# The inverse-total product of the pair attentions moved from VectorE to GpSimd, with shorter runs of unused products

## The reference

```
x = x + attn_a0(norm(x))     16 heads of 64, one key and one value head for all, no mask
x = x + ffn(norm(x))         FP6 blocks of 32, 128 x 128 weight, bias
x = x + attn_a1(norm(x))     16 heads of 64, causal
x = x + ffn(norm(x))
x = x + attn_a2(norm(x))     16 heads over a latent of 32, causal
x = x + experts(norm(x))     top 2 of 8 experts and a shared one
x = x + attn_a3(norm(x))     16 heads of 64, causal, with biases
x = x + experts(norm(x))
attn: softmax(q k^T / 8) v, then the output projection
```

## Time and profile before

| what | value |
|---|---|
| time, median of 3 runs | 2546.32 us (2542.83 to 2547.62) |
| time of the profiled execution | 2549.15 us |
| its span, first to last instruction | 2547.4 us |
| mean granted TensorE clock | 0.982 |
| PE busy | 2461.7 us (97%) |
| DVE busy | 1508.9 us (59%) |
| ACT busy | 1217.3 us (48%) |
| POOL busy | 1263.0 us (50%) |

### The profile page before, as it was taken

The page is one execution under the profiler, slowest core; times in us unless marked ns, Lnnn a source line. Parts: engine busy times, 40 slices in busy tenths (PEclk is TensorE's granted clock), DMA queues, the critical chain, the costliest instruction groups (busy, mean ns, idle before and its releaser), DMA issues. The chain is left out here.

```text
span 2547.4 us, 49159 instructions
## 1 busy us (share of the span) xinstructions
PE 2461.7 (97%) x20265; PEld 1306.2 (51%) x20265; DVE 1508.9 (59%) x2062; ACT 1217.3 (48%) x1830; POOL 1263.0 (50%) x824
## 2 busy tenths in 40 slices
PE   7999999999999999999998999999989999999989
PEld 4444444444444455445546666666554555455545
DVE  5666656777555665556654667666454555555544
ACT  4544545544545555454552344444335554455541
POOL 3877777777766663656543000000006555655530
PEclk9999999999999999999998989999999999999989
DMA  3000000000000000000001100000000000000000
GB/s 85 1 1 1 1 1 1 1 1 1 1 1 1 1 1 1 1 1 1 1 1 23 35 2 3 3 3 3 1 1 1 1 1 1 1 1 1 1 1 17
DMA packets 18658, 13.05 MB, mean 5 GB/s; under 512 B 3074, under 2 KB 17795, under 8 KB 18308
## 3 DMA queue, kind: packets, MB, share of 16 engines
q1 hardware_dynamic: 18436, 9.92, 1.5%
HBM read 8.87 MB, written 1.05 MB: 4 GB/s over the span
## 5 line engine op out<-in xcount | busy, mean ns | idle before, releaser
L1590 POOL TENSOR_TENSOR sums<-sums,p 128x1024 f32<-128x1024 f32 (+3 forms) x384 | 818.8, 2132 | 359.4 <-PE ps L1217 316.2
L1411 DVE TENSOR_REDUCE half_max<-ps 128x2 f32<-128x1024 f32 (+3 forms) x384 | 442.3, 1153 | 381.3 <-PE ps L1196 344.1
L1308 ACT ACTIVATE p<-ps 128x1024 f32<-128x1024 f32 (+3 forms) x384 | 347.7, 916 | 223.3 <-PE ps L1173 164.9
L1170 PE MATMUL ps<-q,k 64*128 64x512 f32 (+3 forms) x1792 | 428.2, 556 | 0.0
L918 POOL TENSOR_TENSOR sums<-sums,p 128x1024 f32<-128x1024 f32 (+3 forms) x160 | 277.5, 1735 | 182.8 <-PE ps L651 166.5
L1217 PE MATMUL ps<-p,v 128*64 128x512 f32 (+3 forms) x1536 | 336.9, 553 | 0.0
L1173 PE MATMUL ps<-max_row,pick 64*128 64x512 f32 (+3 forms) x896 | 326.4, 725 | 0.0
L816 DVE TENSOR_REDUCE half_max<-ps 128x2 f32<-128x1024 f32 (+3 forms) x128 | 130.1, 1019 | 155.2 <-PE ps L630 121.6
L1844 ACT ACTIVATE p<-ps 128x2048 f32<-128x2048 f32 (+1 forms) x80 | 136.5, 1707 | 169.5 <-PE ps L1737 92.0
L1196 PE MATMUL ps<-k_near,q_near 64*128 64x512 f32 (+2 forms) x896 | 195.5, 434 | 21.1 <-DVE half_max L1411 19.2
L1196 PEld LDWEIGHTS ps<-k_near,q_near 64*128 64x128 f32 x896 | 84.6, 186 | 222.8 <-issue 124.5
(11 more groups left out here) (298 smaller groups left out, 4007.7 us busy)
## 6 DMA issues: line engine op xcount, KB each, us to landing
q_w<-in_wq SPq DMA_DIRECT2D x3, 512.0 KB, 5.4
o_w<-in_wo SPq DMA_DIRECT2D x3, 512.0 KB, 8.0
x<-in_x SPq DMA_DIRECT2D x4, 256.0 KB, 3.7
k_w<-in_wk SPq DMA_DIRECT2D x2, 512.0 KB, 6.7
v_w<-in_wv SPq DMA_DIRECT2D x2, 512.0 KB, 7.9
out<-x SPq DMA_DIRECT2D x4, 256.0 KB, 2.3
p<-in_wq_t SPq DMA_DIRECT2D x1, 512.0 KB, 5.1
p<-in_w_out SPq DMA_DIRECT2D x1, 512.0 KB, 7.2
```

The costliest lines, as they stand in the source:

```text
L1170: nc.tensor.matmul(out[:, head, 0:width], a.k[rows, owner(i) % 3, k * P:(k + 1) * P], a.q[rows, i % 3, s * BANK + lo:(s + 1) * BANK], star ...
L1308: act.activation(probabilities(g)[:, :, lo:BANK], score[g % 2][:, :, 0:BANK - lo], ACT.Exp)\
L1411: last = v.tensor_reduce(out, chunk_ps(c)[:, :, 0:hi - lo], AX.X, ALU.max, negate=True)
L1590: pool.tensor_tensor(sums, sums, probabilities(g)[:, :, lo:BANK], ALU.add).then_inc(summed, 1)
```

## The change

- `WARM` goes from 30 to 18, and the counts become: 18 in the opening; 30, 14 and 20 in the norm phase (from 60, 30, 30); 6 in the latent phase (from 15); 3 in each expert phase (from 4).
- In the norm phase POOL's bias addition waits for the quantised values.
- In the three pair attentions `normalise` leaves DVE's list and stands in POOL's, one step earlier, behind the `add_up` of that step. `inverse` has two buffers, so that DVE's spread waits for the product two units back.
- The values of the latent attention's batch 1 move from step 8 to step -3.
- In the expert phases the first gate and up products stand ahead of the router's products of groups 2 and 3.

```
-WARM = 30
+WARM = 18
...
-                pool.wait_ge(normed[g % 2], (g - first) // 2 + 1)
+                pool.wait_ge(quantised, g - first + 1)
...
-            keep_busy(2 * WARM)
+            keep_busy(30)
...
-            keep_busy(WARM)
+            keep_busy(14)
...
-                keep_busy(WARM)
+                keep_busy(20)
...
-                if u >= 1:
-                    dve.wait_ge(normed, u)
-                v.transpose(a.inverse[:].rearrange("p (b q) -> p b q", q=QB),
+                if u >= 2:
+                    dve.wait_ge(normed, u - 1)
+                v.transpose(a.inverse[:, u % 2, :].rearrange("p (b q) -> p b q", q=QB),
                             a.inverses[:].unsqueeze(2).to_broadcast([P, BANK // QB, QB])).then_inc(spread, 1)
-
-            def normalise(i, s):
-                u = unit(i, s)
-                dve.wait_ge(spread, u + 1)
-                dve.wait_ge(mixed_out, u + 1)
-                if u >= 1:
-                    dve.wait_ge(small_mm, use_of["out", (u - 1) // 2, (u - 1) % 2] + 1)
-                v.tensor_tensor(a.mixed[:], a.mixed_raw[:, u % 2, :], a.inverse[:], ALU.mult).then_inc(normed, 1)
...
-                    norms_at[at + 4] = (i, s)
...
-                if g in norms_at:
-                    normalise(*norms_at[g])
...
+            def normalise(i, s):
+                u = unit(i, s)
+                pool.wait_ge(spread, u + 1)
+                pool.wait_ge(mixed_out, u + 1)
+                if u >= 1:
+                    pool.wait_ge(small_mm, use_of["out", (u - 1) // 2, (u - 1) % 2] + 1)
+                pool.tensor_tensor(a.mixed[:], a.mixed_raw[:, u % 2, :], a.inverse[:, u % 2, :], ALU.mult)\
+                    .then_inc(normed, 1)
+
+            norms_at = {begins[i] + when(i)["total", s] + 4: (i, s) for i in range(ITEMS) for s in range(2)}
             for g in range(BEGIN, LAST + 1):
                 if 0 <= g - 1 < TOTAL and step(g - 1)[2] > 0:
                     add_up(g - 1)
+                if g in norms_at:
+                    normalise(*norms_at[g])
...
-                 (("k", 0, 0, -11), ("k", 0, 1, -6), ("v", 0, 0, -4), ("k", 1, 0, -2), ("k", 1, 1, 2), ("v", 1, 0, 8))]
+                 (("k", 0, 0, -11), ("k", 0, 1, -6), ("v", 0, 0, -4), ("v", 1, 0, -3), ("k", 1, 0, -2), ("k", 1, 1, 2))]
...
-                    for _ in range(WARM // 2):
+                    for _ in range(6):
...
-            keep_busy(0, 4)
+            keep_busy(0, 3)
             turn(0, 0)
             for g in range(1, GROUPS):
                 turn(0, g)
+                if g == GROUPS - 1:
+                    gate_and_up(0)
                 route(g - 1)
             route(GROUPS - 1)
-            for i in range(AHEAD - 1):
+            for i in range(1, AHEAD - 1):
```

More of the change, by code:

```diff
@@ L875, in _ @@
                     .then_inc(bias_scaled, 1)
-            turns_at, inverts_at, norms_at = {}, {}, {}
+            turns_at, inverts_at = {}, {}
             for i in range(ITEMS):
@@ L924, in _ @@
             bias_at = {-2: 0, 4: 1, 8: 2, 16: 3}
+            def normalise(i, s):
[6 more added lines that the diff above has]
+                    .then_inc(normed, 1)
+            norms_at = {i * NS + when["total", s] + 4: (i, s) for i in range(ITEMS) for s in range(2)}
             for g in range(BEGIN, LAST + 1):
@@ L1915, in invert @@
                         dve.wait_ge(normed, u)
-                v.reciprocal(a.inverse[:, cols], a.mixed_raw[:, u % 2, QW + half * P:QW + (half + 1) * P])\
+                v.reciprocal(a.inverse[:, 0, cols], a.mixed_raw[:, u % 2, QW + half * P:QW + (half + 1) * P])\
                     .then_inc(inverted, 1)
@@ L1963, in normalise @@
                     pool.wait_ge(small_mm, use_of["out", (u - 1) // UNITS, (u - 1) % UNITS] + 1)
-                pool.tensor_tensor(a.mixed[:, 0:QW], a.mixed_raw[:, u % 2, 0:QW], a.inverse[:, 0:QW], ALU.mult)\
+                pool.tensor_tensor(a.mixed[:, 0:QW], a.mixed_raw[:, u % 2, 0:QW], a.inverse[:, 0, 0:QW], ALU.mult)\
                     .then_inc(normed, 1)
@@ L2349, in build @@
         a.mixed_raw = sb("mixed_raw", [P, 2, BANK])
-        a.mixed, a.total, a.inverse = sb("mixed", [P, BANK]), sb("total", [P, BANK]), sb("inverse", [P, BANK])
+        a.mixed, a.total, a.inverse = sb("mixed", [P, BANK]), sb("total", [P, BANK]), sb("inverse", [P, 2, BANK])
         a.turned, a.inverses = sb("turned", [P, BANK]), sb("inverses", [P, BANK // QB])
```

## The result

| | before | changed kernel |
|---|---|---|
| median, first comparison | 2546.2 us (4 runs) | 2532.3 us (4 runs, 2530.48 to 2534.12) |
| ratio, 95% interval | 1 | 0.9947 (0.993 to 0.9965) |
| profiled execution, its span | 2549.15, 2547.4 us | 2532.78, 2531.0 us |

A second comparison with six more runs of the same changed kernel gave a ratio of 0.9935 (0.9921 to 0.9949). The ten runs of both have a median of 2531.6 us and lie between 2522.5 and 2534.1 us: this spread of 11.6 us is larger than any term of the forecast's sum.

The account below looks back on a forecast made before the run. In the steady part only PE's own work was taken to set the time, with idle or unused products at the joints. Terms -1 + 10 - 2.6 - 10.7 - 8.8 + 0 = -13.1 us gave a 2533.2 us median, range 2525 to 2541.

Parts of the forecast that it names:

- steady pair attentions: Product on POOL at 1.27 us costs 0, hidden; relieved DVE shortens row-maximum waits: 1 us gained, ends 0 and 6.
- two ends: Ends of stream and a3: POOL's products lengthen its addition chain and delay `total`, +5 us each, +10 us together.
- opening: Start of the kernel: 24 fewer rows of unused products, 2.6 us gained.
- norm phase: Shorter fills start DVE's addition at line 389 9.8 us earlier, last fill gains 1 us: together -10.7 us.
- latent phase: Fill -1.9, batch 1 values -2.4, head +1.5, half-clock stretch behind the small products -6: -8.8 us.
- expert phases: One unused product fewer gives 0.9 us each, delayed DVE ranking costs about as much: 0, 2 either way.
- Rival 5: Units where DVE quantises: POOL holds the ports 1.27 us more each, 33 us slower if all reached PE, 2566; chance 0.08.
- POOL's room: Steady units: after the product POOL has some 3 us left per a0 unit, and more room in masked units.
- The last fill: Norm phase's end: 60 rows outlasted the next values by about 1 us; 40 rows are hidden, gaining 1 us.
- Rival 3: Shorter fills keep the clock at half through the norm phase's end and next heads: 2543 us, no change; chance 0.1.
- rival 2: Latent phase drops to half clock elsewhere, for instance its head; the 6 us are not gained: 2539 us; chance 0.19.

Follow-up runs that it names:

- all_dve: Changed kernel with every product of the pair attentions back on DVE, two `inverse` buffers and the other edits kept: 2528.34 us, ratio 0.9924.
- three_more: Changed kernel with the last three products of each stretch on DVE and each of POOL's products made four times over: 2781.32 us in one run.
- latent_third: Kernel before with only the latent phase's edits (6 unused products, batch 1 values at step -3), third traced execution: 2546.26 us.
- norm_latent: Kernel before with the norm phase's and the latent phase's edits together: 2532.06 us, ratio 0.9942.
- latent_alone: Kernel before with only the latent phase's edits (6 unused products, batch 1 values at step -3): 2544.71 us over 11 runs, ratio 0.9987.
- norm_again: Kernel before with only the norm phase's edits (counts 30, 14, 20; bias addition behind the quantised values), traced a second time: 2539.93 us.
- pool_alone: Kernel before with only the product moved to POOL and two `inverse` buffers: 2549.95 us over 11 runs, ratio 1.0014.

## Why the prediction was right, point by point

| term | forecast | traces | by times, alone |
|---|---|---|---|
| steady pair attentions | -1 | -3.8 (waits alone -5.3) | see the ends |
| two ends | +10 | +9.5 | both rows: +3.6 |
| opening | -2.6 | -2.7, -1.5 | with the expert phases -4.6 |
| norm phase | -10.7 | -13.1 | -5.6 |
| latent phase | -8.8 | -7.0 | -3.3, with the norm phase's -14.8 |
| expert phases | 0 | +0.7 (edits -2.2, the end of a3 +2.9) | see the opening |
| sum | -13.1 | -16.4 | -13.5 and -16.6 by the two ratios |

- **The ends** were right in the parts that were counted: `total` 3.96 us later (forecast 4.1), the last product and its hand-over 0.8 (0.7), both alike in a3. Taking them away gave the whole back. Two things were left out. The forecast counted 94 products clear of the ends, but three stand in each end's chain, and PE waits for two of the three. And a later end moves where the next phase meets the clock: in the changed kernel m1 takes 2.9 us more than in `all_dve`, and the norm phase with its projections 1.9 less (33.8 for 35.7 us).
- **The relief of DVE** is the term that was mis-sized: "I take 1 us, with 0 and 6 as ends", because many waits are a round trip through a bank. PE's waits fell by 5.3 us. Nearly all of that lies in the stream, in the units beside which DVE quantises; in a3, where nothing is quantised, it was 0.5. The reasoning was right for a3 and was carried over to the stream. Rival 5, with its blocked ports in just these units, had the sign wrong.
- **POOL's room** in a0 was right: "some 3 us", measured 3.1. The sentence "Masked units are shorter for POOL and have more room" was wrong: their gap ahead of `out` is 3.1 us at its shorter turn, no more than a0's. The forecast's conclusion held, as 1.27 us fit in; how much a product beyond the gap would cost it could not say (`three_more` was expected near 2560 us and took 2781).
- **The norm phase**: 12.2 us for line 389, 9.8 forecast. The latent products and copies took 5.5 us and not 7.1, since the clock fell later, and the transposes and products ran 0.9 us faster than at the half clock that was assumed. The wait was as forecast: 4.03 us for "about 4". The last fill gained 0.95 for 1. Some 0.6 of the 12.2 go with the later end of the stream.
- **The latent phase**: fill -1.9 as forecast; values and the stretch at half behind them -8.49 for -8.4. The head cost 2.9 for 1.5, since it stood at half for 17.1 us.
- **The expert phases** were put at 0, since the wait of the products that moved ahead would eat the gain. With the end of a3 as before, the edits gave 1.5 us in m0 and 0.9 in m1 (`all_dve`).
- **Where the sum held by more than its terms.** Rival 3 (shorter fills let the clock stay at half in the next head) is true of the norm phase's edits alone, and rival 2 (the half clock comes back in the head) of `latent_third`, and by their times of seven of the eleven runs of the latent phase's alone. With both, the middle has no half clock and the head costs 2 to 3 us. The forecast had these as separate terms and came out right with both made; from the same terms it would have forecast each part alone 5 us too fast. That the median came within 1 us or 2 of 2533.2 is in part luck. In the traces the sum is off by 3.3 us, with errors of both signs, and the trace that the terms were read from lies 2.8 us above its kernel's median. It has 13.65 us at half in the latent middle; two others of the four that keep the values there have 3.4, and that middle is 4.5 us shorter in them. So the 6 us of that term are what one kind of execution has to give. Why the head's stretch is short in `norm_latent` (10.2 us), 17.1 in the changed kernel and 23.9 with the norm phase's edits alone stays open.

## What to carry to other kernels

An operation that moves to a slower engine is free only where that engine's own chain has room ahead of the next reader: read the gap for each form of unit, and keep the operation on the fast engine in the last units, where the chain runs without a gap. What a shorter fill of unused products gains can be given back at half clock in the next phase, so measure neighbouring fills together. A gain that rests on the clock's level should be read from several traces of the same program; a single profile was up to 4.6 us off its kernel's median here, and one kernel's runs lie up to 11.6 us apart.

## What the runs showed of the hardware

- POOL's product of 128 x 512 took 1.261 to 1.287 us in all 32 units of a3 and 1.261 to 1.738 in the 64 of the stream, over 1.4 in five of them. DVE's took 0.68 to 2.61 us in the stream, 1.93 in the median, and 0.68 to 2.15 in a3, 1.02 in the median (line 859 of the kernel before). So beside POOL's additions the spread is nearly all on DVE's side. In the stream the product was shorter on POOL than it had been on DVE; in a3 it was not, though it cost nothing there either. The Trainium skill's rule ("GPSIMD Engine Reference", section "4.1 Engine selection"), by which VectorE is the engine for this operation, held where PE waits for the one product: 5 of 96 units.
- Leaving `three_more` aside, the clock was at half for 75 to 116 us of each traced execution, in 11 to 14 stretches (the last of them begins just at the span's end). What a stretch costs depends on where it lies: in the latent head 13.6 us more of it cost 5.5 us (`latent_third` against `latent_alone`), in the latent middle 13.65 us cost some 6 of the 8.49 us that went with it: this is an estimate from `norm_again` and `pool_alone`, where 3.4 us at half made the middle 4.46 us shorter.
